# Exact-split sums for the norms' products with ones, and two DVE instructions between POOL and TensorE

## The chip, the cores and the metric

The program runs on one core of one Trainium2 chip. The metric is the device time of one execution in microseconds (us); the median of several executions is given. The profile comes from one more execution, whose own time stands beside its span.

## The reference, cut to what matters

A stack of four conditioned layers acts on x of shape (4, 512, 512): batch 4, 512 tokens, width 512. Each layer normalizes over the width, and layers 1 and 2 do it twice:

```
L0: mu = mean(x); var = mean((x - mu)**2); h = (x - mu) * rsqrt(var + 1e-5)      # then attention, 16 heads
L1: n = x * rsqrt(mean(x**2) + 1e-6)                                            # before attention and before the MLP
L2: h = (x - mean(x)) / sqrt(var + 1e-6)                                        # before attention and before the MLP
L3: h = layernorm(y) * g + b, with y from 8 small MLPs; then silu and a 512x512 product
```

So there are 6 norms for each of 4 batches: 16 layer norms, which need a mean and then a variance, and 8 RMS norms, which need a mean of squares alone. That makes 40 sums over the width.

## The kernel before

The activations are held with the width on the partitions: x of one batch is 4 tiles (c = 0 to 3) of 128 x 512 (width x tokens). A sum over the width is therefore two steps. POOL (GpSimd) adds the 4 tiles to one in three additions, and TensorE multiplies that tile by a 128 x 128 matrix of 1/512, which sums over the partitions and puts the mean on every partition of a PSUM bank. This product is in fp32. Readers of the bank go on: for a mean DVE's "centre" (L344) subtracts it from the 4 tiles and ACT squares them (L303), for a variance ACT takes "log" (L311) and "inverse" (L316), after which DVE scales (L364) and ACT shifts (L328).

Elsewhere the kernel uses fp32r tiles: a number is kept as a high part, rounded to fp32r, and a low part, and a product is made of three fp32r matmuls (`three`, read at L1213 in the two MLPs). fp32 products are left in the attention, in layers 0, 1 and 3, and in the norms.

Order of the work: each of the four compute engines runs one list of operations, written out in advance. A stage (a norm, a projection, the rotary step) gives its operations as beats, lists of operations that may be issued together. `fold` and `weave` lay the beats evenly behind the main work: the attention of a batch runs in rounds of 4 units (scores, maximum on DVE, exponential on ACT, transposes "turn" on TensorE, copies on ACT and DVE, values), and the beats of the next batch's norm and projection are put at points between them. In the last stage (layer 3) the beats of experts, norm3 and out3 of three batches are merged. An engine takes its list strictly in order: an instruction that waits holds up everything behind it on its engine. Each operation counts up its engine's semaphore, and the others wait for the count (`after`).

In a norm's beats an empty one stands between POOL's additions and the product:

```
tail = [adds, [], [("pe", "var", 0), ("act", "log", 0), ("act", "inverse", 0)]]
return [[("pool", "xsum", i) for i in range(3)], [],
        [("pe", "mean", 0)] + [... ("dve", "centre", c), ("act", "square", c) ...]] + tail + [ends]
```

Names: `k.t1` is the scratch of 4 tiles in which the sums are made; `sb_t` in the profile is this tensor, `sb_hN` the normalized tiles, `sb_Y` the tiles of layer 3, `sb_Pb` the logarithm and the inverse root, `sb_Pr` and `sb_PT` the probabilities and their transposes. norm0, norm1 and norm2 stand before the attentions, norm1b and norm2b before the MLPs, norm3 in the last stage. At the start of the program DVE first reduces the angles of the rotary step (L79 to L91), ACT takes their sines (L98), and both then serve the products that turn the condition into scales and shifts (L132, L138, L152, L167), whose weights arrive by DMA.

Of the kernel before, what the change touches and what calls it, by code (L numbers as in the profile page):

```python
# [10 lines left out]
ALU = mybir.AluOpType  # L11
# [218 lines left out]
class SideNorm:  # L230


    def __init__(s, name, x, h, A, Bias, eps, x_ready, h_free, t_free, rms=False, extra=None, func=None,
                 mod_ready=(), x_loaded=None, high=None, low=None, high_free=()):
        s.x_loaded = x_loaded
        s.high, s.low, s.high_free = high, low, high_free
        s.h, s.func, s.mod_ready = h, func or ACT.Identity, mod_ready
        s.name, s.x, s.A, s.Bias, s.eps, s.rms, s.extra = name, x, A, Bias, eps, rms, extra
        s.x_ready, s.h_free, s.t_free = x_ready, h_free, t_free

    def beats(s, b):
        squares = [("act", "square", c) for c in range(C)]
        scales = [("dve", "scale", c) for c in range(C)]
        adds = [("pool", "vsum", i) for i in range(3)]
        tail = [adds, [], [("pe", "var", 0), ("act", "log", 0), ("act", "inverse", 0)]]
        if s.rms:
            return [squares] + tail + [scales]
        ends = [op for c in range(C) for op in (("dve", "scale", c), ("act", "shift", c))]
        if s.high:
            ends = [op for c in range(C + 1) for op in ([("dve", "scale", c), ("act", "shift", c)] if c < C else []) +  # L250
                    ([("dve", "rest", c - 1)] if c else [])]
        if s.extra:
            ends += [("act", "extra", c) for c in range(C)]
        return [[("pool", "xsum", i) for i in range(3)], [],
                [("pe", "mean", 0)] + [op for c in range(C) for op in (("dve", "centre", c), ("act", "square", c))]] \
            + tail + [ends]

# [2 lines left out]

    def pe(s, k, e, b, kind, i, after):
        bank = s.tab.claim(e, s, b, kind, i, after)
        for due in after(s.name, b, "xsum" if kind == "mean" else "vsum", 2):
            e.wait_ge(*due)
        e.matmul(bank, k.ones[:], k.t1[:, 0, :], start=True, stop=True).then_inc(k.done["pe"], 1)  # L265

    def pool(s, k, e, b, kind, i, after):
        if kind == "xsum" and i < 2:
            if s.x_loaded and i == 0:
                e.wait_ge(*s.x_loaded(b))  # L270
            for c in (2 * i, 2 * i + 1):
                for key in s.x_ready(b, c):
                    for due in after(*key):
                        e.wait_ge(*due)
            for key in s.t_free(b):
                for due in after(*key):
                    e.wait_ge(*due)
            ins = e.tensor_tensor(k.t1[:, i, :], s.x(b, 2 * i), s.x(b, 2 * i + 1), ALU.add)
        elif kind == "vsum" and i < 2:
            for due in after(s.name, b, "square", 2 * i + 1):  # L280
                e.wait_ge(*due)
            ins = e.tensor_tensor(k.t1[:, 2 * i, :], k.t1[:, 2 * i, :], k.t1[:, 2 * i + 1, :], ALU.add)
        else:
            for due in after(s.name, b, kind, 1):
                e.wait_ge(*due)
            other = 1 if kind == "xsum" else 2
            ins = e.tensor_tensor(k.t1[:, 0, :], k.t1[:, 0, :], k.t1[:, other, :], ALU.add)
        ins.then_inc(k.done["pool"], 1)

    def act(s, k, e, b, kind, c, after):  # L290
# [44 lines left out]
        ins.then_inc(k.done["act"], 1)  # L335

    def dve(s, k, e, b, kind, c, after):
        if kind == "centre":
            for due in after(s.name, b, "mean", 0):
                e.wait_ge(*due)  # L340
            for key in s.h_free(b):
                for due in after(*key):
                    e.wait_ge(*due)
            ins = e.tensor_tensor(s.h(b, c), s.x(b, c), s.tab.at[(s.name, b, "mean", 0)], ALU.subtract)  # L344
        elif kind == "rest":
            for due in after(s.name, b, "shift", c):
                e.wait_ge(*due)
            ins = e.scalar_tensor_tensor(out=s.low(b, c), in0=s.h(b, c), scalar=s.Bias(b, c),
                                         in1=s.high(b, c).bitcast(F32), op0=ALU.add, op1=ALU.subtract)
        else:  # L350
            for due in after(s.name, b, "inverse", 0):
                e.wait_ge(*due)
            if s.rms:
                for key in s.h_free(b):
                    for due in after(*key):
                        e.wait_ge(*due)
            else:
                for due in after(s.name, b, "square", c):
                    e.wait_ge(*due)
            for key in s.mod_ready:  # L360
                for due in after(*key):
                    e.wait_ge(*due)
            src = s.x(b, c) if s.rms else s.h(b, c)
            ins = e.scalar_tensor_tensor(out=s.h(b, c), in0=src, scalar=s.A(b, c), in1=k.rstd,  # L364
                                         op0=ALU.mult, op1=ALU.mult)
        ins.then_inc(k.done["dve"], 1)
# [927 lines left out]
def conditioned_stack(nc, a, out):  # L1294
    ctx = ExitStack()
    with ctx:
# [11 lines left out]
        x = sb("x", [P, C, B, T])  # L1308
        with ExitStack() as scope:
            hNlow = scope.enter_context(nc.sbuf_tensor("sb_hNlow", [P, C, T], F32R))  # L1310
            scope.enter_context(nc.sbuf_tensor("sb_t1_offset", [P, C, T], F32))
            k.rootparts = scope.enter_context(nc.sbuf_tensor("sb_rootparts", [P, 2, T], F32R))
        k.hN = sb("hN", [P, C, T])
        k.t1 = sb("t1", [P, C, T])
        k.Pb = sb("Pb", [P, 2, T])
        k.sd, k.rstd = k.Pb[:, 0, :], k.Pb[:, 1, :]
        k.ident = sb("ident", [P, P])
        k.ones = sb("ones", [P, P])
        k.strip = sb("strip", [P, 32])
        k.lesser = sb("lesser", [P, 1])  # L1320
        k.freq = sb("freq", [P, 1])
# [78 lines left out]
        l_x = [sem(f"l_x{b}") for b in range(B)]  # L1400
        l_first, l_rope, l_cols, l_cond = sem("l_first"), sem("l_rope"), sem("l_cols"), sem("l_cond")
        l_ada = [sem(f"l_ada{i}") for i in range(3)]
        k.s_angle, l_wo0 = sem("s_angle"), sem("l_wo0")
        l_w = [sem(f"l_w{i}") for i in range(2)]
        l_w3 = sem("l_w3")
# [48 lines left out]
        def wide(name):  # L1454
# [9 lines left out]
        n_cols = len(COLS) + 2  # L1464
        BLOCKS = ADA * P // D
        ada = Ada(cond, lambda j: wada[j % 3], lambda j: (l_ada[j % 3], 16 * (j // 3 + 1)), ada_rows, sel[:], mod, modb,
                  [float(j in (0, 2, 3, 6, 7, 10)) for j in range(BLOCKS)], combs, (l_first, 16 * 6),
                  (l_cols, 16 * n_cols), (l_cond, 16))
        angles = Angles()

# [505 lines left out]
        def _(e):  # L1976
# [2 lines left out]
            for b in range(B):  # L1979
                e.dma_start(k.pos[32 * b:32 * b + 32, :], a["pos"][b].partition_broadcast(32)).then_inc(k.l_pos, 16)  # L1980
            e.dma_start(k.ident[:], a["ident"]).then_inc(l_first, 16)
            e.dma_start(k.ones[:], a["ones"]).then_inc(l_first, 16)
            e.dma_start(sel[:], a["sel"]).then_inc(l_first, 16)
            e.wait_ge(s_zero, 4)
            for name, t0, n in MODB:
# [15 lines left out]
        def _(e):  # L2001
            e.memset(eps5[:], 1e-5).then_inc(s_zero, 1)
            e.memset(eps6[:], 1e-6).then_inc(s_zero, 1)
            e.memset(cond[:], 0.0).then_inc(s_zero, 1)
            e.memset(modb[:], 0.0).then_inc(s_zero, 1)
            engine(e, "dve", 0, len(phases))

        @block.scalar
# [84 lines left out]
```

## Time and profile before

| | |
|---|---|
| median of 3 runs | 2404.7 us (2399.85 to 2404.94) |
| profiled execution | 2398.59 us, span 2396.8 us, mean granted TensorE clock 0.98 |
| TensorE (PE) busy | 2244.7 us, 94% |
| DVE busy | 1168.9 us, 49% |
| ACT busy | 1033.6 us, 43% |
| POOL busy | 292.5 us, 12% |
| instructions | 34593 |

How to read it: busy is the time in which at least one instruction of the engine was under way. An fp32 matmul shows as two records, an fp32r matmul as one. Matmul records overlap, so the pace of TensorE is read from start to start, or from the chain of waits, in which each record counts from the end of the one before. In a row of instructions the bracket gives the idle time of the engine just before it and what ended it.

### The profile page before, as it was taken

How to read it: one execution, taken by the hardware profiler on the slowest of the kernel's cores; microseconds unless marked ns; L12 is line 12 of the kernel's file. 1: busy time of each engine (PE TensorE's matmuls, PEld its weight loads, DVE VectorE, ACT ScalarE, POOL GpSimd, SP SyncE). 2: the span in 40 equal slices, each digit the busy share in tenths (PEclk: the TensorE clock that was granted, in tenths of full speed). 3: DMA queues.
4: the chain of work that ended last, by engine and by line, in shares of the span. 5: the costliest groups of instructions: out<-in, count | busy, mean ns of one | idle time of the engine just before them, and what ended most of it. 6: DMA issues, size and time to landing. Idle time of an engine off the chain costs nothing.

```text
span 2396.8 us, 34593 instructions
## 1 busy us (share of the span) xinstructions
PE 2244.7 (94%) x14034; PEld 1511.1 (63%) x14034; DVE 1168.9 (49%) x2499; ACT 1033.6 (43%) x2425; POOL 292.5 (12%) x246
## 2 busy tenths in 40 slices
PE   5889999999999999999999989999999989999998
PEld 2455555555555687888877756565664668888633
DVE  2345454454457344433443356657587554544322
ACT  2355555444446221111113366657676552222473
POOL 3331122122021001110001010101010110000021
PEclk9889999999999999999999999999999999999999
DMA  8310020000010002110102211011110101100001
GB/s 274 113 40 27 15 64 26 23 23 18 18 40 27 31 27 84 54 61 27 36 6 79 79 53 67 31 63 36 54 36 19 53 1 36 36 1 1 1 18 53
DMA packets 59487, 104.97 MB, mean 44 GB/s; under 512 B 10592, under 2 KB 24560, under 8 KB 59328
## 3 DMA queue, kind: packets, MB, share of 16 engines
q1 hardware_dynamic: 58368, 100.30, 12.6%
q0 software_dynamic: 960, 2.45, 0.3%
q8 instruction: 111, 1.82, 0.3%
q14 instruction: 48, 0.39, 0.1%
HBM read 77.04 MB, written 10.49 MB: 37 GB/s over the span
## 4 chain that ended last, share of the span: by engine, by line
PE 84%; ACT 7%; DVE 6%; POOL 1%; issue 1%; SPq 1%; DMA 1%; DVEq 0%; POOLq 0%; ACTq 0%
PE banks L1213 36%; PE banks L404 22%; PE banks L740 6%; PE banks L732 4%; PE banks L756 4%; ACT sb_Pr L842 2%; PE banks L766 2%; PE banks L265 1%; ACT sb_PT L847 1%; PE banks L906 1%; DVE sb_hN L364 1%; PE banks L630 1%; PE banks L638 1%; DVE sb_Pr L812 1%; PE banks L890 1%
## 5 line engine op out<-in xcount | busy, mean ns | idle before, releaser
L1213 PE MATMUL banks<-sb_HH,sb_Ws 128*128 128x512 f32 x1536 | 490.2, 392 | 12.7 <-DVE sb_HL L1103 7.3
L1213 PEld LDWEIGHTS banks<-sb_HH,sb_Ws 128*128 128x128 f32 x1536 | 289.6, 189 | 76.7 <-issue 16.7
L1213 PE MATMUL banks<-sb_hidH,sb_Ws 128*128 128x512 f32 x1024 | 331.2, 392 | 0.4 <-DVE sb_x L1284 0.4
L842 ACT ACTIVATE sb_Pr<-sb_Pr,sb_nmax 128x512 f32<-128x512 f32 (+4 forms) x512 | 291.6, 576 | 30.9 <-DVE sb_nmax L812 30.8
L1213 PE MATMUL banks<-sb_HL,sb_Ws 128*128 128x512 f32 x768 | 300.0, 391 | 0.0
L847 ACT ACTIVATE sb_PT<-banks 128x512 f32<-128x512 f32 (+2 forms) x320 | 143.5, 496 | 302.6 <-PE banks L740 225.5
L740 PEld LDWEIGHTS banks<-sb_ident,sb_Pr 128*128 128x128 f32 x1536 | 169.7, 142 | 125.5 <-issue 38.9
L819 DVE COPY sb_PT<-banks 128x512 f32<-128x512 f32 (+2 forms) x320 | 168.6, 563 | 163.1 <-PE banks L740 108.7
L740 PE MATMUL banks<-sb_ident,sb_Pr 128*128 128x128 f32 x1536 | 214.2, 282 | 18.2 <-DVE sb_A L830 5.0
L1213 PEld LDWEIGHTS banks<-sb_hidH,sb_Ws 128*128 128x128 f32 x1024 | 192.3, 188 | 44.0 <-issue 2.5
L1213 PE MATMUL banks<-sb_hidL,sb_Ws 128*128 128x512 f32 x512 | 199.4, 389 | 0.0
L404 PE MATMUL banks<-sb_A,sb_W 128*128 128x512 f32 x384 | 176.8, 604 | 3.8 <-DVE sb_x L1488 2.4
L812 DVE CUSTOM_DVE_ANT_0 sb_Pr<-banks,sb_bias 128x512 f32<-128x512 f32 x256 | 161.5, 686 | 32.9 <-PE banks L732 32.8
L1265 DVE TENSOR_TENSOR sb_tiles<-sb_tiles,banks 128x512 f32<-128x512 f32 x64 | 44.0, 687 | 262.0 <-PE banks L1213 262.0
L1240 ACT ACTIVATE sb_hidH<-sb_tiles 128x512 fp32r<-128x512 f32 x128 | 81.0, 633 | 197.2 <-DVE sb_tiles L1265 195.2
L1213 PEld LDWEIGHTS banks<-sb_HL,sb_Ws 128*128 128x128 f32 x768 | 144.9, 189 | 30.7 <-issue 1.0
L404 PE MATMUL banks<-sb_hN,sb_W 128*128 128x512 f32 x320 | 150.5, 615 | 4.9 <-ACT sb_hN L328 2.8
L1235 ACT ACTIVATE sb_tiles<-banks,sb_cols 128x512 f32<-128x512 f32 x64 | 44.1, 689 | 237.4 <-PE banks L1213 237.4
L732 PE MATMUL banks<-sb_R 32*128 32x512 f32 (+1 forms) x768 | 143.6, 635 | 1.6 <-DVE sb_R L591 0.8
L1284 DVE SCALAR_TENSOR_TENSOR sb_x<-banks,sb_mod,sb_x 128x512 f32<-128x512 f32 x128 | 95.9, 750 | 90.2 <-PE banks L1213 89.9
L1232 ACT ACTIVATE sb_tiles<-banks 128x512 f32<-128x512 f32 x64 | 38.2, 598 | 219.9 <-PE banks L1213 219.8
L1271 DVE TENSOR_TENSOR sb_hidL<-sb_tiles,sb_hidH 128x512 fp32r<-128x512 f32 x128 | 88.5, 692 | 77.7 <-ACT sb_hidH L1240 77.6
(160 smaller groups left out, 3251.7 us busy)
## 6 DMA issues: line engine op xcount, KB each, us to landing
sb_ring<-split_units SPq DMA_DIRECT2D x48, 512.0 KB, 3.3
sb_ropet<-sb_R SPq DMA_DIRECT2D x70, 128.0 KB, 2.0
sb_staged<-in_L_cond_Wfc SPq DMA_DIRECT2D x16, 512.0 KB, 4.6
sb_wada<-in_L_cond_Wada SPq DMA_DIRECT2D x6, 1024.0 KB, 5.5
split_units<-sb_unitpair SPq DMA_DIRECT2D x12, 512.0 KB, 2.9
sb_x<-in_x SPq DMA_DIRECT2D x4, 1024.0 KB, 9.1
sb_staged<-in_L_cond_Wg SPq DMA_DIRECT2D x8, 512.0 KB, 3.7
sb_staged<-in_L_cond_Wu SPq DMA_DIRECT2D x8, 512.0 KB, 4.7
```

The lines of the kernel that those rows point to most:

```text
L404: mm = e.matmul(out, lhsT, rhs, start=start, stop=stop)
L732: mm = e.matmul(bank[:, 0:s.width(u)], s.q(b, c)[rows, i * P:(i + 1) * P], s.k(b, c)[rows, 0:s.width(u)], start=True, stop=True)
L740: mm = e.transpose(bank[:, j * P:(j + 1) * P], k.Pr[:, n % 6, j * P:(j + 1) * P], k.ident[:])
L756: mm = e.matmul(bank[rows, 2 * P * ip + skip:2 * P * (ip + 1)], s.v(b, j, s.vhead(c, hl)), s.PT[:, n % 2, hl, j, skip:2 * P], start=j == 0 ...
L812: ins = e.tensor_tensor_reduce(k.Pr[:, n % 6, 0:s.width(u)], S, s.bias[:, s.units[u][2], 0:s.width(u)], -1.0, 3.0e38, ALU.add, ALU.min, s. ...
L819: ins = e.tensor_copy(*s.turned(k, b, u))
L842: ins = e.activation(prob, prob if s.biased else k.bank(n % 4)[:, 0:s.width(u)], ACT.Exp, bias=s.stat(k, k.nmax, b, u), scale=-1.0 if s.bi ...
L847: ins = e.activation(*s.turned(k, b, u), ACT.Copy)
L1213: mm = e.matmul(bank, lhsT, rhs, start=i == 0, stop=i == len(mats) - 1)
L1240: ins = e.activation(k.hidH[:, st % 2, t, :], k.tile(t), ACT.Copy)
L1271: ins = e.tensor_tensor(k.hidL[:, st % 2, t, :], k.tile(t), k.hidH[:, st % 2, t, :].bitcast(F32), ALU.subtract)
L1284: ins = e.scalar_tensor_tensor(out=k.xs(q, m), in0=s.tab.at[(s.name, b, "down", index)], scalar=1.0 if s.gamma is None else s.gamma(q, m), ...
```

## The change

All 40 sums are given to TensorE as two fp32r tiles, and the product with ones is two fp32r matmuls into the same bank in place of one fp32 product.

- POOL makes the same three additions. The first two now leave their results in tiles 0 and 2 of `k.t1`; the third writes its result rounded to fp32r, into tile 1 under the name `k.t1parts` (the same memory as `k.t1`, seen as fp32r).
- DVE has two new instructions for each sum, "xrest" or "vrest" 0 and 1, both 128 x 512 with two SBUF inputs: tile 2 = tile 2 - rounded sum, then tile 0 = tile 2 + tile 0, which is what the rounding left over. They stand in the beat that was empty. The second waits for the first.
- TensorE waits for the second rest (before: for POOL's third addition) and multiplies tile 0 and tile 1 by the ones.
- The matrix of ones is loaded to another tile with a semaphore of its own (`l_ones`), and DVE copies it to fp32r. The wait for this load and the copy are DVE's first work after its four fills, ahead of the angles. The load stays where it was among POOL's issues.
- Nothing else changes: the beats, the banks, ACT's work and all other products are the same.

```diff
         adds = [("pool", "vsum", i) for i in range(3)]
-        tail = [adds, [], [("pe", "var", 0), ("act", "log", 0), ("act", "inverse", 0)]]
+        tail = [adds, [("dve", "vrest", i) for i in range(2)],
+                [("pe", "var", 0), ("act", "log", 0), ("act", "inverse", 0)]]
...
-        return [[("pool", "xsum", i) for i in range(3)], [],
+        return [[("pool", "xsum", i) for i in range(3)], [("dve", "xrest", i) for i in range(2)],
...
     def pe(s, k, e, b, kind, i, after):
         bank = s.tab.claim(e, s, b, kind, i, after)
-        for due in after(s.name, b, "xsum" if kind == "mean" else "vsum", 2):
+        if b == 0:
+            e.wait_ge(k.s_ones, 1)
+        for due in after(s.name, b, "xrest" if kind == "mean" else "vrest", 1):
             e.wait_ge(*due)
-        e.matmul(bank, k.ones[:], k.t1[:, 0, :], start=True, stop=True).then_inc(k.done["pe"], 1)
+        e.matmul(bank, k.ones[:], k.t1parts[:, 1, :], start=True, stop=False)
+        e.matmul(bank, k.ones[:], k.t1parts[:, 0, :], start=False, stop=True).then_inc(k.done["pe"], 1)
...
-            ins = e.tensor_tensor(k.t1[:, i, :], s.x(b, 2 * i), s.x(b, 2 * i + 1), ALU.add)
+            ins = e.tensor_tensor(k.t1[:, 2 * i, :], s.x(b, 2 * i), s.x(b, 2 * i + 1), ALU.add)
...
-            other = 1 if kind == "xsum" else 2
-            ins = e.tensor_tensor(k.t1[:, 0, :], k.t1[:, 0, :], k.t1[:, other, :], ALU.add)
+            ins = e.tensor_tensor(k.t1parts[:, 1, :], k.t1[:, 0, :], k.t1[:, 2, :], ALU.add)
...
     def dve(s, k, e, b, kind, c, after):
-        if kind == "centre":
+        if kind in ("xrest", "vrest"):
+            if c == 0:
+                for due in after(s.name, b, kind[0] + "sum", 2):
+                    e.wait_ge(*due)
+                ins = e.tensor_tensor(k.t1[:, 2, :], k.t1[:, 2, :], k.t1parts[:, 1, :].bitcast(F32), ALU.subtract)
+            else:
+                for due in after(s.name, b, kind, 0):
+                    e.wait_ge(*due)
+                ins = e.tensor_tensor(k.t1parts[:, 0, :], k.t1[:, 2, :], k.t1[:, 0, :], ALU.add)
+        elif kind == "centre":
...
-            scope.enter_context(nc.sbuf_tensor("sb_t1_offset", [P, C, T], F32))
+            k.t1parts = scope.enter_context(nc.sbuf_tensor("sb_t1parts", [P, C, T], F32R))
...
-        k.ones = sb("ones", [P, P])
+        with ExitStack() as scope:
+            k.ones_read = scope.enter_context(nc.sbuf_tensor("sb_ones_read", [P, P], F32))
+        k.ones = sb("ones", [P, P], F32R)
...
+        l_ones, k.s_ones = sem("l_ones"), sem("s_ones")
...
-                  [float(j in (0, 2, 3, 6, 7, 10)) for j in range(BLOCKS)], combs, (l_first, 16 * 6),
+                  [float(j in (0, 2, 3, 6, 7, 10)) for j in range(BLOCKS)], combs, (l_first, 16 * 5),
...
-            e.dma_start(k.ones[:], a["ones"]).then_inc(l_first, 16)
+            e.dma_start(k.ones_read[:], a["ones"]).then_inc(l_ones, 16)
...
             e.memset(modb[:], 0.0).then_inc(s_zero, 1)
+            e.wait_ge(l_ones, 16)
+            e.tensor_copy(k.ones[:], k.ones_read[:]).then_inc(k.s_ones, 1)
             engine(e, "dve", 0, len(phases))
```

## Rows read from the trace of the kernel before

**Rows 1.** The page: busy time of the engines; the chain that ended last, by engine.

```profile
PE 2244.7 (94%) x14034; PEld 1511.1 (63%) x14034; DVE 1168.9 (49%) x2499; ACT 1033.6 (43%) x2425; POOL 292.5 (12%) x246
...
PE 84%; ACT 7%; DVE 6%; POOL 1%; issue 1%; SPq 1%; DMA 1%; DVEq 0%; POOLq 0%; ACTq 0%
```

**Rows 2.** Groups of instructions: line, operation, shapes, count, busy us, mean ns, idle before.

```profile
L265 PE MATMUL banks<-sb_t,sb_ones 128*128 128x512 f32 x80 | 47.4, 677 | 11.2 <-POOL sb_t L287 11.2
...
L1271 DVE TENSOR_TENSOR sb_hidL<-sb_tiles,sb_hidH 128x512 fp32r<-128x512 f32 x128 | 88.5, 692 | 77.7 <-ACT sb_hidH L1240 77.6
...
L287 POOL TENSOR_TENSOR sb_t<-sb_t 128x512 f32<-128x512 f32 x40 | 51.6, 1290 | 3.1
```

**Rows 3.** The chain of waits, 1885 to 1960 us: start, us, piece.

```profile
1904.19 0.86 PE banks L265 x2
1905.05 6.82 PE banks L1213 x30
...
1936.85 1.28 ACT L50
```

**Rows 4.** The chain of waits at the start, 0 to 100 us.

```profile
3.44 7.95 DMA sb_A<-in_pos
...
29.39 1.93 PE banks L265 x2
...
37.24 2.08 PE banks L265 x2
```

**Rows 5.** Timeline, 0 to 45 us: start, us, engine, line, instruction.

```profile
4.50 0.54 POOL L1982 DMA_DIRECT2D sb_ones<-in_ones  x1
...
11.42 0.43 DVE L79 CAST sb_A<-sb_A 128x512 f32<-128x512 int32 x1 [10.17 <-DMA sb_A<-in_pos]
```

**Rows 6.** DMA issues: KB each, us from issue to landing.

```profile
sb_ones<-in_ones POOLq DMA_DIRECT2D x1, 64.0 KB, 7.3
```

**Rows 7.** Timeline of DVE, 165 to 171 us (layer 0, batch 0's attention, norm0 of batch 2).

```profile
167.30 0.75 DVE L819 COPY sb_PT<-banks 128x256 f32<-128x256 f32 x2
168.63 0.36 DVE L812 CUSTOM_DVE_ANT_0 sb_Pr<-banks,sb_mask 128x193 f32<-128x193 f32 x1 [0.58 <-PE banks L899]
```

**Rows 8.** Timeline of POOL, 168 to 174 us.

```profile
172.06 1.26 POOL L287 TENSOR_TENSOR sb_t<-sb_t 128x512 f32<-128x512 f32 x1
```

**Rows 9.** Timeline of DVE, 1919 to 1954 us (start of layer 2's MLP).

```profile
1929.04 0.69 DVE L1271 TENSOR_TENSOR sb_hidL<-sb_tiles,sb_hidH 128x512 fp32r<-128x512 f32 x1
...
1933.35 0.82 DVE L1271 TENSOR_TENSOR sb_hidL<-sb_tiles,sb_hidH 128x512 fp32r<-128x512 f32 x1
```

**Rows 10.** Timeline of POOL, 1932 to 1938 us.

```profile
1932.33 3.00 POOL L282 TENSOR_TENSOR sb_t<-sb_t 128x512 f32<-128x512 f32 x2 [9.55 <-ACT sb_t L303]
```

**Rows 11.** Timeline of DVE, 1504.5 to 1511 us (layer 2's attention).

```profile
1504.69 1.28 DVE L819 COPY sb_PT<-banks 128x512 f32<-128x512 f32 x2
...
1508.33 2.48 DVE L344 TENSOR_TENSOR sb_hN<-sb_x,banks 128x512 f32<-128x512 f32 x4
```

**Rows 12.** The chain of waits in the last stage.

```profile
2313.69 1.06 PE banks L265 x2
...
2359.52 1.27 POOL sb_t L287
...
2360.84 1.13 PE banks L265 x2
...
2368.83 0.86 PE banks L265 x2
```

**Rows 13.** Timeline of DVE, 2357 to 2375 us.

```profile
2368.87 0.75 DVE L1731 SCALAR_TENSOR_TENSOR sb_x<-banks,sb_cols,sb_x 128x512 f32<-128x512 f32 x1 [2.68 <-PE banks L404]
2373.16 0.75 DVE L1731 SCALAR_TENSOR_TENSOR sb_x<-banks,sb_cols,sb_x 128x512 f32<-128x512 f32 x1 [3.54 <-PE banks L404]
```

**Rows 14.** Stretches: busy us of PE, PEld, DVE, ACT, POOL, then granted clock and DMA.

```profile
90.00:280.00 190.00, 161.60 (x1722) 98.64 (x1722) 95.16 (x394) 106.65 (x384) 50.72 (x40) 0.90 0.09 27
...
460.00:640.00 180.00, 177.04 (x1011) 98.79 (x1009) 86.48 (x142) 78.63 (x194) 33.52 (x26) 1.00 0.06 21
...
1500.00:1640.00 140.00, 132.33 (x1070) 85.14 (x1070) 91.24 (x216) 90.93 (x215) 11.36 (x9) 1.00 0.14 46
...
1760.00:1885.00 125.00, 112.30 (x991) 67.27 (x990) 90.97 (x213) 91.55 (x212) 18.96 (x15) 0.96 0.08 26
```

## The prediction

> **What bounds the kernel now.** I read the page first. TensorE is busy 94% of the span and carries 84% of the chain that ended last, DVE is at 49% and ACT at 43% [rows 1]. So time taken off a TensorE product counts almost everywhere, and the question is what the new DVE work does to the moments at which TensorE may start. The groups come next: the 40 products with ones are 80 records (L265), and TensorE stood idle only 11.2 us in all for POOL's last addition [rows 2]. Third, the chain of waits gives the pace of both kinds of matmul. Last, I laid the order of the operations beside the timelines, and for each of the 40 places noted three moments: when POOL's third addition ends, when DVE is done with the operation in front of the formerly empty beat, and when the product starts.
>
> **What is saved.** In the chain an fp32 product with ones takes 0.86 us, and 30 fp32r matmuls take 6.82 us, 0.227 each [rows 3]. Two in place of a product: 0.455, a saving of 0.41 us. With the clock at half, as in the first 40 us, the product took 1.93 and 2.08 us [rows 4]; I take 1.0 saved there, and 0.85 for three more at half clock in the first attention, a stretch with a mean clock of 0.90 [rows 14]. Sum: 35 x 0.41 + 2 x 1.0 + 3 x 0.85 = 18.9 us. POOL's additions keep their number and size.
>
> **What is added.** 80 DVE instructions of 128 x 512 with two SBUF inputs. The nearest row is L1271, same shape and inputs, 692 ns [rows 2]. A pair, with 0.04 for the second's wait, is 1.42 us; from the end of POOL's addition to the start of the product I count 1.46 where before it was 0.05. DVE gets 57 us more. What one pair costs depends on three things: does TensorE reach the product before the rests are done; does DVE, in order, reach the beat before POOL has finished, so that everything behind waits too; and is DVE full there.
>
> *The start.* DVE's first work waited for the positions, until 11.42 [rows 4, 5]. The ones are issued later, at 4.50 to 5.04, and take 7.3 us [rows 5, 6]: landing between 11.8 and 12.3. With a copy of some 0.2 us (an eighth of the 128 x 2048 copies' size and more for the fixed part; bounds 0.1 and 0.4) the angles start 0.6 to 1.3 us late, and they are on the chain: I take 0.9. The first mean saves 1.0, since its rests fit before TensorE comes; the first variance product waited on POOL, so it pays 1.4 and saves 1.0. Together +0.3.
>
> *norm0, batches 1 to 3, beside the first attention.* Five of six products start late enough after the rests; they save about 3. The exception: the variance of batch 2. DVE passes the beat's place at 168.05 (167.30 + 0.75) and goes on with maxima at 168.63 [rows 7], while POOL's third addition ends at 173.32 [rows 8]. DVE would now stand from 168.05 to 174.7, and behind it stand four maxima and so the next four scores, which need their banks: these started at 172.3, and now wait for rests (173.32 + 1.42) and maxima (four in 1.16), until 175.9: 3.6 us later. Net with the added DVE work: +0.5 (bounds -1.5 and +4).
>
> *norm1, four batches.* TensorE is 98% busy and DVE half [rows 14], and the sums are done 8 to 20 us before the product. Pure saving: -1.6.
>
> *norm1b and norm2's first batch.* norm1b: at three of its four the product starts within 0.05 to 1.3 us of the sum. Each pays about 1.4 and saves 0.41: +2.9. Its last one and the two of norm2's batch 0 lie in the MLP with room (DVE is idle for microseconds there) and only save 0.41 each. So +2.5 for norm1b and -0.8 for norm2's first.
>
> *norm2, batches 1 to 3, and norm2b, 0 and 1, beside the second attention.* Here DVE and ACT are each busy 65 to 73% [rows 14], and around a norm DVE has no gap: copies from 1504.69 to 1505.97, four maxima, then centres from 1508.33 to 1510.81 [rows 11]. A pair in front moves centres, squares and sums by about 1.2 us; following the copies and maxima to the next places where TensorE waits for a bank gives about 1.7 us of wait for TensorE in a norm, against 0.82 that its two products save. I take +0.9 for each of three and +0.7 for each of the two in the emptier last stretch, +4.1 (bounds -3, if all is absorbed, and +10, if both pairs count in full: 5 x (2.84 - 0.82)).
>
> *norm2b, batches 2 and 3.* For the mean of batch 3 DVE ends the operation in front of the beat at 1929.73 (1929.04 + 0.69), while the product started at 1927.61, two microseconds earlier [rows 9]. The rests can only follow. The path after them is a chain without slack (centre, squares, sums, product, table load [rows 3], log, scale, shift, pair), at whose end TensorE already stands idle. Both pairs and their shift arrive there: +2.75 (bounds +1 and +5).
>
> *norm3, the last stage.* In two of eight places the product started right after POOL's last addition, as at 2360.84 after 2359.52 + 1.27 [rows 12], and waits the full 1.4 us more. In five more DVE's put of out3 comes immediately before the beat, and the rests can only follow it: for the last variance the put ends at 2369.62 (2368.87 + 0.75), the product began at about 2368.7, and would now begin at 2371.1 [rows 12, 13]. Adding the waits one after another, with the 0.41 taken off each time, the shift grows to 0.9 after norm 0, 1.6 after norm 1, 2.4 after norm 2, and 5.6 after norm 3, whose two products lie on the chain to the end. +5.6 (bounds +3 and +8).
>
> **The sum.** 0.3 + 0.5 - 1.6 + 2.5 - 0.8 + 4.1 + 2.75 + 5.6 = +13.35 us, that is some 32 us of waits against 18.9 saved. For the profiled execution 2398.6 becomes 2412; the median was 6.1 us above it, so I forecast 2418 us.
>
> **A rule about the port.** When a DVE instruction of this kind ran beside POOL's additions, two additions took 3.00 us (a single one elsewhere 1.26 [rows 8]), and DVE's instruction 0.82 instead of 0.69 [rows 9, 10]. The Trainium skill, "SBUF — State Buffer", section "SBUF: two separate sides", states that DVE and GpSimd share a port pair as an exclusive lock, held for the whole instruction, also by a DVE instruction with two SBUF inputs. By that rule, the trace agrees. In this change the rests run when POOL's own chain has ended, so the norms' additions are not hit; POOL's rotary instructions behind them can be, by 0.5 us each, in the 12 norms of the first two attentions. They have slack, and I book nothing; if all counted it would be 16 x 0.5 = 8 us.
>
> **Rivals.**
> 1. *No change: the attentions absorb theirs.* ACT and TensorE run on while DVE makes rests, and the rounds have room for them. The second attention then gives -3 in place of +4.1, norm0 -1.5 in place of +0.5, norm1b +1 in place of +2.5, and the last stage and the MLP's start stay: +2.8, 2407 us. For it: DVE is idle a third of the second attention and half of the first [rows 14]. Against it: it has no gap just where the pair goes in [rows 11]. Chance 0.15.
> 2. *Faster: only POOL's old waits grow.* At eight places the product started within 0.25 us of POOL's addition, which also hold all of the 11.2 us idle time [rows 2]. If these alone pay, 8 x 1.41 = 11.3 against 18.9 saved: -7.6, 2397 us. It decides once the waits in all stay under 14 us. For it: in the mean a product had microseconds to spare. Against it: the places where DVE itself comes late [rows 7, 9, 13]. Chance 0.11.
> 3. *DVE fills up.* In the second attention both pairs count in full (+6 more), and DVE's stand of 6.7 us in norm0 goes through whole (+4), and the clock falls to half behind it for a while (+1), and rotary instructions are blocked (+3): +14 more, +27, 2432 us. Chance 0.13.
> 4. *The fp32r product with ones isn't at 0.227 us a matmul.* Then nothing is saved: +32, 2437 us. Against it: 30 matmuls of this kind and shape in a row hold that pace [rows 3]. Chance 0.02.
>
> The forecast has 0.59. A difference under 0.2% (4.8 us) can't be told from no change in this kernel. The forecast's own range is 2411 to 2426. 2402 to 2430 takes in rival 1 and leaves out rival 2, about half of rival 3 and rival 4, 0.19 together. Slower by over 0.2%: the forecast but for the end of its lower tail (0.58), rivals 3 and 4, and a little of rival 1: 0.74. Within 0.2%: most of rival 1 and a little of the forecast: 0.14. Faster: rival 2 and the rest of rival 1: 0.12.
>
> **What the profile after would show.** L265: 80 records at 0.227 to 0.43 us from start to start, busy time well below 47.4 us. Idle time of TensorE before L265 from under 12 to some 25 us, now ended by DVE's rest. DVE busy about 1225 us. A DVE wait of about 5 us for POOL near 168 us. The first DVE instruction on the angles near 12.3. The last stage 5 to 6 us longer from 2265 to the end. I am wrong if TensorE's idle time before the products stays near 11 us, if the second attention doesn't grow, or if the last stage is no longer than before.

## The result: slower by 1.1%, twice the forecast

| | before | changed |
|---|---|---|
| median of 4 runs each | 2403.4 us (2399.9 to 2404.9) | 2430.5 us (2422.5 to 2434.5) |
| ratio | | 1.011 (95% interval 1.0093 to 1.0127) |
| profiled execution, span, granted clock | 2398.6, 2396.8, 0.98 | 2434.5, 2432.7, 0.973 |

The forecast was 2418 us (+13), the measurement says +27: above the forecast's own range of 2411 to 2426, and just above the wider one that ends at 2430. The page of the changed kernel, busy time, granted clock and the chain by engine, against [rows 1]:

```profile
PE 2248.9 (92%) x14034; PEld 1521.8 (63%) x14034; DVE 1221.8 (50%) x2580; ACT 1034.9 (43%) x2425; POOL 294.7 (12%) x246
...
PEclk8888999999999999999999999999999999999999
...
PE 80%; DVE 9%; ACT 6%; POOL 2%; issue 1%; DMA 1%; SPq 1%; DVEq 0%; POOLq 0%; ACTq 0%
```

DVE's busy time grew by 53 us and its part of the chain from 6 to 9%. TensorE's busy time did not fall, though 40 products became shorter. Groups of instructions of the changed kernel, as in [rows 2]:

```profile
L291 POOL TENSOR_TENSOR sb_t1parts<-sb_t 128x512 fp32r<-128x512 f32 x40 | 51.7, 1292 | 3.1
L346 DVE TENSOR_TENSOR sb_t<-sb_t,sb_t1parts 128x512 f32<-128x512 f32 x40 | 29.8, 745 | 23.4 <-POOL sb_t1parts L291 23.4
...
L350 DVE TENSOR_TENSOR sb_t1parts<-sb_t 128x512 fp32r<-128x512 f32 x40 | 28.6, 716 | 1.4
L269 PE MATMUL banks<-sb_t1parts,sb_ones 128*128 128x512 f32 x40 | 22.6, 566 | 31.6 <-DVE sb_t1parts L350 31.4
L270 PE MATMUL banks<-sb_t1parts,sb_ones 128*128 128x512 f32 x40 | 18.6, 465 | 0.0
```

Two waits are new, or longer. TensorE stands idle 31.6 us before L269, now for the rests, against 11.2 for POOL's sum [rows 2]. And DVE stands 23.4 us for POOL before its first rest (L346), at ten places; I had named one of them. The 80 rests take 58.4 us, close to the 55 that the nearest row gave.

**Where the time went.** I matched TensorE's operations one by one between two traces and read how far each is shifted; the table gives what the shift gains in each stretch. The last column does so with a second pair of profiles (the experiments e8 and e11 below, each kernel once more):

| stretch (us of before) | forecast | shift gained, first pair | second pair |
|---|---|---|---|
| start, to 90 | +0.3 | +2.0 | +2.7 |
| first attention with norm0 1 to 3, to 350 | +0.5 | +9.7 | +6.5 |
| norm1, to 640 | -1.6 | +2.9 | +0.1 |
| norm1b, to 900 | +2.5 | +2.5 | +2.0 |
| MLP, norm2 batch 0, to 1380 | -0.8 | +0.9 | -2.2 |
| second attention, to 1885 | +4.1 | +5.1 | +8.5 |
| start of layer 2's MLP, to 2265 | +2.75 | +5.6 | +5.7 |
| last stage | +5.6 | +7.2 | +7.1 |
| sum | +13.35 | +35.9 | +30.4 |

The sizes differ between the pairs by up to 3.4 us in a stretch, which matters below.

**The stand in norm0.** Timelines of DVE and of POOL in the changed kernel, where [rows 7] and [rows 8] are from:

```profile
169.90 0.75 DVE L832 COPY sb_PT<-banks 128x256 f32<-128x256 f32 x2
175.49 1.73 DVE L346 TENSOR_TENSOR sb_t<-sb_t,sb_t1parts 128x512 f32<-128x512 f32 x1 [4.84 <-POOL sb_t1parts L291]
177.26 0.69 DVE L350 TENSOR_TENSOR sb_t1parts<-sb_t 128x512 fp32r<-128x512 f32 x1
177.87 0.35 DVE L825 CUSTOM_DVE_ANT_0 sb_Pr<-banks,sb_mask 128x193 f32<-128x193 f32 x1
```

```profile
174.20 1.26 POOL L291 TENSOR_TENSOR sb_t1parts<-sb_t 128x512 fp32r<-128x512 f32 x1
175.42 1.26 POOL L494 TENSOR_TENSOR sb_R<-sb_R,sb_cos 128x512 f32<-128x512 f32 x1
```

And TensorE's next scores behind it, in its timeline:

```profile
178.29 1.41 PE L903 MATMUL banks<-sb_R 32*128 32x128 f32 x6 [3.71 <-DVE sb_nmax L825]
```

DVE stands 4.84 us with maxima behind it whose scores have long been made, and TensorE then stands 3.71 us for these maxima. The first rest takes 1.73 us and not 0.69: POOL's rotary instruction (L494) begins 0.07 us before it. The rest ends 0.54 us after that one does.

**The last stage.** The chain of waits of the changed kernel, from norm3's last mean to its last variance, beside [rows 12]:

```profile
2389.59 1.27 POOL sb_t1parts L291
2390.86 0.03 issue
2390.89 0.70 DVE sb_t L346
...
2391.62 0.70 DVE sb_t1parts L350
...
2392.36 0.80 PE banks L269
2393.16 0.43 PE banks L270
2393.59 9.24 PE banks L417 x16
2402.83 0.03 issue
2402.85 0.75 DVE sb_x L1747
2403.61 0.61 DVE sb_t L346
...
2404.24 0.70 DVE sb_t1parts L350
...
2404.98 0.78 PE banks L269
```

The chain runs through both rests, as forecast. But the 16 matmuls of out3 between the two products take 9.24 us here, 9.43 in TensorE's timeline. Before, the same 16, between the products at 2360.84 and 2368.83 [rows 12], took 7.03 in the timeline. The stretch of these two products in the kernel before (columns as in [rows 14]):

```profile
2353.00:2378.00 25.00, 20.66 (x49) 8.42 (x49) 11.53 (x17) 12.74 (x18) 6.28 (x5) 0.96 0.22 84
```

and in the changed kernel, under its stretch of the first attention:

```profile
92.00:292.00 200.00, 169.60 (x1722) 106.08 (x1722) 103.88 (x406) 106.68 (x384) 50.96 (x40) 0.85 0.08 25
...
2384.60:2411.00 26.40, 20.58 (x40) 8.58 (x36) 9.74 (x16) 9.53 (x13) 6.28 (x5) 0.81 0.11 40
```

The granted clock around the two products is 0.81 against 0.96: after the stand of 3.06 us before L269 TensorE was at the lower of its two levels (1.2 of 2.4 GHz) for part of the stretch. The 8 matmuls behind the last product take 4.82 us against 3.60. At the very end it is the other way round: the last 32 matmuls of the program, before and then in the changed kernel:

```profile
2375.47 15.67 PE L404 MATMUL banks<-sb_Y,sb_Wout 128*128 128x512 f32 x32 [2.35 <-ACT sb_Y L328]
```

```profile
2413.07 14.00 PE L417 MATMUL banks<-sb_Y,sb_Wout 128*128 128x512 f32 x32 [2.26 <-ACT sb_Y L332]
```

In the first attention the granted clock is 0.85 against 0.90 [rows 14]. So a stand can be paid twice, once idle and once in the matmuls behind it. That became the theory to test, beside the rival that DVE's added load is the cost and the waits only show it.

### The profile page after: what moved, and what is told of

Its sections match the earlier page's. It is cut to its first block, busy times and chain, and to the rows that moved or that the text cites. A ratio compares the mean times of both kernels' runs of the same rounds, so it can differ in the third digit from the quotient of the medians.

```text
span 2432.7 us, 34671 instructions
## 1 busy us (share of the span) xinstructions
PE 2248.9 (92%) x14034; PEld 1521.8 (63%) x14034; DVE 1221.8 (50%) x2580; ACT 1034.9 (43%) x2425; POOL 294.7 (12%) x246
## 4 chain that ended last, share of the span: by engine, by line
PE 80%; DVE 9%; ACT 6%; POOL 2%; issue 1%; DMA 1%; SPq 1%; DVEq 0%; POOLq 0%; ACTq 0%
PE banks L1226 35%; PE banks L417 22%; PE banks L753 6%; PE banks L745 4%; PE banks L769 4%; DVE sb_Pr L825 2%; PE banks L779 1%; ACT sb_Pr L855 1%; PE banks L919 1%; DVE sb_hN L377 1%; ACT sb_PT L860 1%; PE banks L651 1%; PE banks L903 1%; PE banks L643 1%; ACT sb_x L338 1%
## 5 line engine op out<-in xcount | busy, mean ns | idle before, releaser
L1226 PEld LDWEIGHTS banks<-sb_HH,sb_Ws 128*128 128x128 f32 x1536 | 290.1, 189 | 78.3 <-issue 17.6
L417 PE MATMUL banks<-sb_hN,sb_W 128*128 128x512 f32 x320 | 153.2, 624 | 6.6 <-ACT sb_hN L332 2.8
L769 PE MATMUL banks<-sb_PT,sb_V 128*32 128x256 f32 (+1 forms) x1536 | 125.3, 388 | 0.0
```

The costliest lines, as they stand in the source:

```text
L417: mm = e.matmul(out, lhsT, rhs, start=start, stop=stop)
L769: mm = e.matmul(bank[rows, 2 * P * ip + skip:2 * P * (ip + 1)], s.v(b, j, s.vhead(c, hl)), s.PT[:, n % 2, hl, j, skip:2 * P], start=j == 0 ...
L1226: mm = e.matmul(bank, lhsT, rhs, start=i == 0, stop=i == len(mats) - 1)
```

## The experiments

The edits are to the changed kernel, except for e11. `split_sum` in them chooses which sums are split; the others keep the fp32 product, no rests, and an empty beat. "Come back" below is the changed kernel's median of 2430.5 less the experiment's. From the spread of the runs (4 to 6 of an experiment, 8 of the changed kernel with e8) I estimate that such a difference is good to some 5 us either way, and the kernel before had medians of 2401.5 to 2404.7 beside the experiments.

**e1, no rests.** DVE's two instructions are gone, TensorE waits for POOL's sum and multiplies it twice. This leaves out the rests, so the kernel does not compute the reference:

```diff
-        tail = [adds, [("dve", "vrest", i) for i in range(2)],
+        tail = [adds, [],
...
-        for due in after(s.name, b, "xrest" if kind == "mean" else "vrest", 1):
+        for due in after(s.name, b, "xsum" if kind == "mean" else "vsum", 2):
...
-        e.matmul(bank, k.ones[:], k.t1parts[:, 0, :], start=False, stop=True).then_inc(k.done["pe"], 1)
+        e.matmul(bank, k.ones[:], k.t1parts[:, 1, :], start=False, stop=True).then_inc(k.done["pe"], 1)
```

> Leaves out both rests: TensorE waits for POOL's third addition as before the change and multiplies the rounded sum twice (so every mean is doubled and has no rest). DVE's 80 instructions and their latency are gone; the fp32r products and the copy of the ones at the start stay. Theory A (the saving is real, the loss is waits and the clock): 2403 - 19 + 1 = 2385 us, 2380 to 2391. Rival B (two fp32r matmuls with ones save little beside their neighbours): 2396 to 2404.

Measured: 2391.6 us, ratio 0.996 (0.9945 to 0.9974), between the two expectations. The short products alone are worth 9.9 us, half of what either the forecast or theory A gave them. The stretch of the first attention in e1 has no rests at all, and yet a granted clock of 0.88, where the kernel before has 0.91 from 90 to 290 us:

```profile
90.00:290.00 200.00, 170.57 (x1826) 105.79 (x1827) 97.65 (x407) 110.60 (x397) 52.33 (x41) 0.88 0.09 26
```

**e2, rests made but not waited for.** DVE does all of its work in its place; TensorE starts on POOL's sum and multiplies it twice, as in e1, and the next batch's additions wait for the rests:

```diff
-        for due in after(s.name, b, "xrest" if kind == "mean" else "vrest", 1):
+        for due in after(s.name, b, "xsum" if kind == "mean" else "vsum", 2):
...
-        e.matmul(bank, k.ones[:], k.t1parts[:, 0, :], start=False, stop=True).then_inc(k.done["pe"], 1)
+        e.matmul(bank, k.ones[:], k.t1parts[:, 1, :], start=False, stop=True).then_inc(k.done["pe"], 1)
...
-            for key in s.t_free(b):
+            for key in s.t_free(b) + ([(s.name, b - 1, "vrest", 1)] if b else []):
...
```

> The rests are made at the same places in DVE's order, but TensorE doesn't wait for them: it waits for POOL's third addition and multiplies the rounded sum twice (every mean doubled, no rest). The next batch's first writer of the scratch waits for the rests. It separates DVE's load and its standing still in order from the latency in front of the product. Theory A: DVE's stand near 168 us and its full stretches remain (about +8 with the clock behind it), the latency goes: 2390 to 2405. Rival C (DVE's load as such is nearly all of the loss): 2415 to 2430. Rival D (all of the loss is the latency in front of the products): 2383 to 2389.

Measured: 2412.9 us, ratio 1.0045 (1.0029 to 1.0061), 21.3 above e1. I had expected about 8 from DVE's part (2390 to 2405 us), rival C 2415 to 2430; the measurement lies between, nearer to the rival. The waits of TensorE in e2, by what it waited for (us in total, times, longest):

```profile
PE banks L269 <- POOL sb_t1parts L291: 12.4, 6, 3.1
```

TensorE's wait at the products is back at 12.4 us, and DVE's at L346 is still 23.1 us. So 21.3 of the 39 us between e1 and the changed kernel don't come from TensorE waiting for rests, and the waiting adds the other 17.6 us (15.7 if each kernel is set against the kernel before of its own session). The 21.3 come from what the rests do in DVE's queue. Matched as above, one profile each, e2 falls behind e1 by 4.9 us in the first attention and by 14.0 in the second, and by nothing in the last stage; there the changed kernel falls 9.7 behind e2. So in the attentions mostly DVE's queue is paid, and in the last stage the wait of TensorE. The wait that e2 adds for POOL explains none of this: POOL stood for it at norm3 alone, in the last stage.

**e3, norm0 of batches 1 to 3 whole.**

```diff
+def split_sum(name, b, kind):
+    return name != "norm0" or b == 0
```

> Only norm0's batches 1 to 3 (6 of 40 sums, in the first attention) go back to the fp32 product and have no rests; the other 34 are as after the change. Theory A (DVE's stand near 168 us and the half clock behind it cost some 8 us there): 2418 to 2424. Rival E (these six cost what any six do, 27 us x 6 / 40 = 4 us, or save by themselves): 2426 to 2432.

Measured: 2423.8 us, ratio 1.0093 (1.0074 to 1.0112), so 6.7 us come back, in the range of theory A; with some 5 us either way this does not exclude rival E.

**e4, only where there is room.** 11 of 40 sums are split, and the ones are copied after the angles:

```diff
+    return name == "norm1" or (name, b) in (("norm2", 0), ("norm1b", 3)) or (name, b, kind) in (("norm0", 0, "x"), ("norm0", 1, "v"), ("norm0", 3, "x"), ("norm0", 3, "v"))
```

> Split sums only where the trace shows room on DVE and in front of the product: norm1's four, norm2's two of batch 0, norm1b's of batch 3, norm0's first mean, its variance of batch 1 and both of batch 3: 11 of 40. The ones are copied after the angles. Theory A: 11 x 0.41 and some at half clock = -5 to -6 us, 2396 to 2400, faster than both kernels. Rival C (DVE's load costs wherever it is put): 2403 to 2412.

Measured: 2405.4 us, ratio 1.001 (0.9996 to 1.0023). A miss: no gain, and a time in the range of rival C. In its trace the stretch from 190 to 280, with norm0 of batch 3, is 3.0 us longer than before, though the products there start microseconds after their rests are done.

**e5, the ends whole.** norm3's eight sums and norm2b's of batches 2 and 3:

```diff
+    return name != "norm3" and (name, b) not in (("norm2b", 2), ("norm2b", 3))
```

> The last stage's eight sums (norm3) and the four of norm2b's batches 2 and 3 go back to the fp32 product without rests; the other 28 are as after the change. Theory A (these chains cost 5.6 + 2.75 us by my sum, 13 us by the trace after): 2415 to 2423. Rival F (the trace's last stretches only show the shift of one execution): 2426 to 2432.

Measured: 2417.8 us, ratio 1.0051 (1.0036 to 1.0066); 12.7 us come back, as theory A said.

**e6, rests one beat later.** One more empty beat stands before the rests, so that DVE does other work first:

```diff
-        tail = [adds, [("dve", "vrest", i) for i in range(2)],
+        tail = [adds, [], [("dve", "vrest", i) for i in range(2)],
...
```

> After the change, with one more empty beat between POOL's additions and the rests (the product one beat later as well). DVE should no longer stand still for POOL in the attentions, the products come later in the order. Theory A: it takes back what DVE's stands cost in the attentions (5 to 10 us) and loses a little in the last stage, where a beat is work of TensorE: 2418 to 2427. Rival C (DVE's load): unchanged, 2427 to 2433.

Measured: 2426.3 us, ratio 1.0087 (1.0069 to 1.0105), 4 us under the changed kernel, which is within the noise: the interval overlaps that of e8. TensorE's wait at the products fell to 24.6 us, but DVE's stands in front of the rests only from 23.4 to 19.3 us.

**e7, ones copied after the angles.**

```diff
+            e.wait_ge(k.l_ones, 16)
+            e.tensor_copy(k.ones[:], k.ones_read[:]).then_inc(k.s_ones, 1)
             return
...
-            e.wait_ge(l_ones, 16)
-            e.tensor_copy(k.ones[:], k.ones_read[:]).then_inc(k.s_ones, 1)
             engine(e, "dve", 0, len(phases))
```

> After the change, with the wait for the ones and their copy moved behind DVE's angles (after the sine's negation), where DVE waits for TensorE anyway. Theory A: takes back the 0.66 us that the first product with the condition comes late, and no more: 2428 to 2431. Rival G (the late start shifts the clock's and the DMAs' phases and costs several us): 2420 to 2426.

Measured: 2430.4 us, ratio 1.0103 (1.0085 to 1.0121). No difference: the order at the start is worth nothing that can be measured, and rival G is out.

**e8, the changed kernel again.** No edit.

> The kernel after the change once more, unchanged, on the same chip as e5 to e7: a second trace of it. 2422 to 2435 as before. If the shift by stretch repeats (first attention +8 to +10, second +4, start of the second MLP +5 to +6, last stage +7), the stretches' shares are those of the change; if the first attention's share differs by several us at the same median, the half clock behind a wait is chance in part.

Measured: 2431.0 us, ratio 1.0103 (1.0086 to 1.0119).

**e9, the stand in norm0 undone.** Only the variance of norm0's batch 2 is whole:

```diff
+    return (name, b, kind) != ("norm0", 2, "v")
```

> The whole change, but for one sum: the variance of norm0's batch 2 keeps the fp32 product and has no rests. This is the one place in the first attention where DVE stands until POOL is done. Theory A (that single stand carries most of what norm0 costs there): the four scores at 172 start 3.6 us earlier than in the changed kernel, the jump of 3.6 at that place is gone, and the median is 3 to 4 us under the changed kernel's 2430.5: 2426 to 2428. Theory B (it is a load spread over all of norm0, and TensorE at half clock for longer): the jump goes, but the time comes back by the end of the stretch at 280, and the median is 2429 to 2432.

Measured: 2423.4 us, ratio 1.0085 (1.007 to 1.01). 7.1 us come back from one sum of 40, more than either theory gave; with some 5 us either way, the 3 to 4 us of theory A are not excluded. DVE at that place, against the stand above:

```profile
169.52 0.75 DVE L844 COPY sb_PT<-banks 128x256 f32<-128x256 f32 x2
170.85 0.36 DVE L837 CUSTOM_DVE_ANT_0 sb_Pr<-banks,sb_mask 128x193 f32<-128x193 f32 x1 [0.58 <-PE banks L924]
```

and the stretch of the first attention in e9:

```profile
92.00:292.00 200.00, 171.74 (x1796) 105.72 (x1800) 102.97 (x413) 109.81 (x394) 51.92 (x40) 0.88 0.08 26
```

The scores behind it start 4.2 us earlier than in the changed kernel (174.13 against 178.29; 0.4 us of it come from before the place), and TensorE's operations at 276 us of the kernel before are 6.9 us earlier. The granted clock of the stretch is 0.88 in place of 0.85; but e8, with the stand, has 0.87, and e2, with the same stand of DVE, 0.88. e3, which undoes five more sums, takes back no more in the median.

**e10, five sure places.** norm1's four variances and norm1b's last; the rest as before, the ones copied after the angles:

```diff
+    return name == "norm1" or (name, b) in (("norm1b", 3),)
```

> Only five of the 40 sums are split (norm1's four variances and norm1b's last), those that the trace of before gave as sure savings; the other 35 keep the fp32 product and have no rests, and the ones are copied after the angles. Theory A (each saves its 0.41 us): 2 us under the kernel before, ratio 0.999, 2400 to 2403. Theory B (a TensorE product saved in the middle is taken back at the next place where a load, DVE or ACT ends the wait): no difference, ratio 1.000, and the stretch from 460 to 640 us shows at most 1 us less. In no case should it be slower than before by over 1 us; if it is, the products with ones set the start at the table of the angles or the clock does more than I think.

Measured: 2399.2 us, ratio 0.9984 (0.9972 to 0.9995). It computes all of the reference and is 3.8 us under the kernel before. Theory A said 2; the interval holds both, and reaches from 1 to 7 us.

**e11, the kernel before again.** No edit.

> The kernel before, unchanged, profiled once more. The profiled execution of before stood 5 us under its median, that of the changed kernel 4 us over its own. If the jumps of TensorE's operations at 274, 364 and 933 us, which nearly all experiments show against the first profile (1.5 + 3.6 + 1.3 to 2 us, even without any rests), come from that profile's luck, this one shows them too. If they come from the change, this one lies within 1 us of the first profile everywhere.

Measured: 2404.4 us, span 2402.6. TensorE's operations run 5.8 us later at the end than in the first profile. The changed kernel and nearly all experiments show three jumps against the first profile, at 364, 933 and 274 us. Those at 364 and 933 us are here too, that at 274 is not. The first is a wait for a weight load, in the timeline of TensorE in e11:

```profile
360.25 5.37 PE L404 MATMUL banks<-sb_hN,sb_W 128*128 128x512 f32 x8 [1.51 <-DMA sb_W<-in_L_cond_Wq]
```

In the first profile of before the same 8 matmuls take 3.60 us and don't wait. The other is in the MLP. One stretch of the same kernel in its two profiles, the first and then e11:

```profile
925.00:950.00 25.00, 22.27 (x98) 18.15 (x98) 12.26 (x16) 2.91 (x5) 4.99 (x5) 1.00 0.34 116
```

```profile
925.00:950.00 25.00, 22.27 (x86) 17.81 (x85) 9.24 (x14) 2.72 (x5) 3.80 (x4) 0.86 0.32 116
```

In both TensorE stands 2.73 us for DVE's weights (L1257); in one the clock stays at 1.00, in the other it falls to 0.86, and the matmuls behind are 2.3 us later. So a stand of the same length is followed by the lower clock in one execution and not in another.

**e12, the middle whole.** norm1b 0 to 2, norm2 1 to 3 and norm2b 0 and 1, 13 sums:

```diff
+    return not ((name == "norm1b" and b < 3) or (name == "norm2" and b > 0) or (name == "norm2b" and b < 2))
```

> The sums between the first attention and layer 2's MLP that pay for their rests are whole again: norm1b of batches 0 to 2, norm2 of batches 1 to 3, norm2b of batches 0 and 1, 13 sums in all; norm0, norm1, norm3 and the rest stay as changed. Theory A (the forecast's own terms, 2.9 and 4.1 us): 7 us come back, 2423 to 2424. Theory B (the parts must close the sum: 27 us over the kernel before, of which 7 came back with norm0's stand and 13 with the two ends, and the five sure savings are worth 3 to 4): 9 to 12 us come back, 2418 to 2422. Theory C (with DVE's stand of norm0 upstream the middle's waits are hidden, and the pieces don't add up): under 4 us, 2427 to 2431.

Measured: 2420.6 us, ratio 1.0072 (1.0055 to 1.0089); 9.9 us come back, as theory B said. Two stretches of the second attention, in the changed kernel and then in e12:

```profile
1518.70:1660.70 142.00, 131.97 (x1069) 84.87 (x1068) 94.08 (x220) 91.43 (x216) 11.35 (x9) 1.00 0.14 46
1781.90:1908.10 126.20, 111.47 (x991) 66.48 (x990) 95.61 (x221) 91.85 (x212) 18.99 (x15) 0.97 0.08 26
```

```profile
1509.90:1649.90 140.00, 132.34 (x1070) 85.05 (x1070) 91.21 (x216) 90.92 (x215) 11.36 (x9) 1.00 0.14 46
1769.90:1895.00 125.10, 112.46 (x991) 66.98 (x990) 90.97 (x213) 91.61 (x212) 18.95 (x15) 0.96 0.08 26
```

With the sums whole they have their 140 and 125 us of before [rows 14]; the pairs of rests cost 2.0 us for the one norm and 1.1 us for the two. Here the clock does not differ, and the cost is what DVE's queue adds.

## Why the forecast had the sign and half of the size

**The books.** Four numbers from each trace: the span; TensorE's idle time (span less busy time); what the clock held back, (1 - granted clock) x span; and the 40 products, each from its start to the start of the next operation. For seven products of the kernel before, in the MLPs, I added 0.4 us: there the record of the next matmul starts 0.03 us after the product's second record, but the one behind it comes 0.4 us late. Before and changed are means of their two profiles. The clock is known to three digits, so its column is good to about 1 us.

| | span | idle | held back by the clock | products |
|---|---|---|---|---|
| before | 2399.7 | 153.2 | 50.4 | 43.0 |
| e1, no rests | 2388.2 (-11.5) | +4.3 | -0.2 | -16.3 |
| e2, rests not waited for | 2413.0 (+13.3) | +13.2 | +14.8 | -15.0 |
| changed | 2432.9 (+33.2) | +30.1 | +16.5 | -13.8 |

In each row the last three add up to the change of the span within 1 us. That is in part chance: idle time at the lower clock is counted in two columns, and so is what products at the lower clock take longer. The forecast had one column of waits, 32 us of them, close to the 30.1 of idle time. It had no column for the clock, which took 16.5.

**By experiments**, in medians: the stand in norm0 7.1 (e9), the middle 9.9 (e12), the ends 12.7 (e5), together 29.7, each good to some 5 us. The whole is 27.1, so start and sure places are worth -2.6 (e10, which keeps five of the sure ones, measured -3.8). The forecast's terms for the same groups are +0.5, +7.0, +8.35 and -2.5. So it is these:

- *norm0, the step that failed.* The prediction found the stand and its first price: DVE from 168.05 to 174.7, the scores 3.6 us later. Measured are a stand of 4.84 us, and scores 3.8 us later in both pairs (the forecast read their old start as 172.3 us; the trace has 171.91). The failing step was "net with the added DVE work: +0.5". The 3 us taken off did not arrive: in e1 the stretch from 90 to 350 has all of the short products and no rests, and is 0.1 us longer than before, at a granted clock of 0.88 against 0.91. And the price did not stay 3.6: up to 350 us the shift grows by another 5.1 us in the first pair and 3.2 in the second, where e9 has 2.5; e9 gives 7.1 for the stand in the medians. That maxima and copies behind it are late too is seen in the timelines. How much the clock adds here stays open: its values with and without the stand (0.85 and 0.87; 0.88) lie too close to those of e1 and e2 (0.88).
- *The products, a mis-sized term.* I took 18.9 us off; the starts show 13.8. A pair stands at 0.236 + 0.234 us at only three places, all in the MLP. Among short matmuls it is 0.314 + 0.326 against 0.432 + 0.522 before, 0.31 saved and not 0.41. Even where it is shorter, the time need not be: in e1 the products are 16.3 us shorter and the median 9.9, with 4.3 us more idle time. And 12 of the 40 pairs ran at the lower clock, against 6 products before: there a pair behind a stand takes 0.594 + 0.427 = 1.02 us, a little more than the fp32 product at full clock (0.96).
- *The last stage, a mis-sized term.* +5.6 forecast, 7.2 measured, inside its bounds of 3 and 8. The waits were at the places named: the product after the sum, and the variance behind DVE's put. What the sum lacked is out3's clock: 2.4 us for the 16 matmuls, 1.2 for the next 8, and 1.7 back at the last 32, 1.9 in all. The other 5.3 are near the 5.6, but split otherwise: 1.4 up to norm3 of the last batch, where 2.4 was told, and more behind it. In e9 the same 16 matmuls take 8.11 us, so the clock's part varies.
- *The start of layer 2's MLP*: +2.75 forecast, 5.6 measured, just over the bound of +5. The mean of batch 3 came as told, and two variances, whose DVE stands of 1.9 us I had not seen, follow it.
- *norm1*: -1.6 forecast, +2.9 and +0.1 found up to 640 us. From 460 to 640, where two of its four products lie, the shift falls by 0.8 us in both pairs and in e1 and e10, so the saving arrives as told; between its two profiles the kernel before, unchanged, differs by 1.6 us from 350 to 640. For norm2's first batch, -0.8 against +0.9 and -2.2, the pairs say nothing.
- *norm1b and second attention*: 2.5 forecast and 2.5 and 2.0 found; 4.1 and 5.1 to 8.5, inside the bounds. e12 gives 9.9 for both against 7.0.
- *The start*: the angles started at 12.58 (forecast 12.3), and the stretch is 2 us longer, but e7 shows that it doesn't matter to the median. The copy took 0.23 us; by its size it is a sixteenth of the 128 x 2048 copies and not, as the forecast has it, an eighth. The timeline of DVE:

```profile
12.43 0.23 DVE L2023 CAST sb_ones<-sb_ones_read 128x128 fp32r<-128x128 f32 x1 [11.18 <-DMA sb_ones_read<-in_ones]
12.58 0.42 DVE L79 CAST sb_A<-sb_A 128x512 f32<-128x512 int32 x1
```

- *The rule about the port.* I had booked nothing, on the ground that the rests run when POOL's chain has ended. What I had not seen is that POOL goes straight on to a rotary instruction, and then it is the rest that is long: 1.73 us against 0.69, at a place where everything waits. Three pairs of the 40 were lengthened so, by 1.4, 1.0 and 0.6 us over 1.41, two more by 0.1. By the rule in the Trainium skill, "SBUF — State Buffer", section "SBUF: two separate sides", this is what a lock held by POOL looks like, and the trace agrees: the rest ended 0.54 us after POOL's instruction, and the first rests of the other two pairs 0.55 us after theirs.
- *The rivals.* The third, DVE fills up and the clock falls, gave 2432 us for a chance of 0.13 and is nearest to the measurement. That is luck in part: its stand that goes through whole is borne out (7.1 us for 0.5 + 4), but of its 6 us more in the second attention the pairs show 1 to 4, what the port held up were mostly rests (3.0 us over three pairs, where POOL's busy time grew by 2.2), and its 1 us for the clock is far from the 16.5 of the books. That the attentions absorb the pairs (rival 1) is refuted by e2 and e12, and the faster case (rival 2) by the idle time before L269.

**What stays open.** e2 over e1 is 9 us more idle and 15 us more held back by the clock, and no run separates these two. Why the six further sums of e4 cost 6 us over e10, when their products had room, is shown only in part: 3 us in the stretch of norm0's batch 3. The clock's part as a whole is read from the books; whether it falls after a given stand isn't told by its length here (e11), and no experiment steered it. A form with the rests on POOL wasn't tried.

## What to carry to other kernels

Price helper work on an in-order engine by what stands behind it, not by who waits for its result: here 21 us were paid with TensorE not waiting for the result at all, most of it in the attentions, where DVE has no gap. Of 16.3 us shorter products 9.9 arrived (e1). I read that as: a saving arrives only where TensorE is what ends the wait. Count it from start to start among its real neighbours, and give it only to places where both the producer and the helper's queue have room (five of 40 here, worth 0.16%, with an interval from 0.05 to 0.28%). And where TensorE's stands grow, add the slower matmuls behind them: in this kernel the clock held back 16.5 us beside 30.1 of idle time.

## What the runs showed of the hardware

- The same kernel with the same stand of 2.73 us kept the clock at 1.00 in one execution and fell to 0.86 over 25 us in another. This gives a difference of 2.3 us between two profiles at one place, and a profile pair alone (35.9 us) can overstate the change in medians (27.1).
- A pair of fp32r matmuls of 128x512 at the lower clock, behind a stand, takes 1.02 us, no less than the fp32 product at full clock (0.96).
- A DVE instruction of 0.69 us that began 0.07 us after one of POOL's (1.26 us) took 1.73 us, and ended 0.54 us after POOL's.
